# A two-layer AdaLN transformer on one core: the order of work in layer 1's feed-forward at its entry, pair change and end, and four operand rests on GpSimd

## What is computed

```python
h = _layernorm(x) * (1 + cb) + sb
g = (h @ gate_w.T) * gate_s          # 1408 hidden units
u = (h @ up_w.T) * up_s
x = x + gb * (((silu(g) * u) @ down_w.T) * down_s)
```

## Time and profile before

| | |
|---|---|
| median of three runs | 1994.6 us |
| the profiled execution | 1995.5 us, its span 1993.7 us |
| TensorE (PE) busy | 1905.1 us, 96% of the span |
| VectorE (DVE), ScalarE (ACT), GpSimd (POOL) busy | 58%, 35%, 39% |
| granted TensorE clock, mean | 0.986 of 2.4 GHz |

### The profile page before, as it was taken

One profiled execution on the slowest core, in us unless ns is written; L12 is line 12 of the kernel. 1 busy time (PEld: TensorE's weight loads), 2 busy tenths in 40 slices (PEclk: granted clock), 3 DMA queues, 4 the chain that ended last, 5 costly groups with the idle time before them and its releaser, 6 DMA issues. The chain is left out here.

```text
span 1993.7 us, 26372 instructions
## 1 busy us (share of the span) xinstructions
PE 1905.1 (96%) x9936; PEld 1367.3 (69%) x9936; DVE 1163.8 (58%) x1948; ACT 707.2 (35%) x1275; POOL 775.3 (39%) x730
## 2 busy tenths in 40 slices
PE   7999999999999999899999999998998878998998
PEld 5677555544555545788888888887886667776887
DVE  5466877666666733854434443445333767777776
ACT  4221355545555564521111111114221244343332
POOL 1122778788776589200000000002001556664662
PEclk9999999999999999999999999999999989999999
DMA  9852422322321203200001010002000011111211
GB/s 326 267 150 107 97 54 55 86 55 55 86 45 33 60 19 99 69 33 32 32 1 32 32 32 1 1 19 74 6 6 11 22 32 53 54 48 43 95 54 48
DMA packets 80783, 120.83 MB, mean 61 GB/s; under 512 B 7008, under 2 KB 38768, under 8 KB 80624
## 3 DMA queue, kind: packets, MB, share of 16 engines
q1 hardware_dynamic: 73200, 93.96, 16.5%
q0 software_dynamic: 7456, 25.18, 4.2%
HBM read 93.68 MB, written 25.44 MB: 60 GB/s over the span
## 5 line engine op out<-in xcount | busy, mean ns | idle before, releaser
L1795 DVE TENSOR_REDUCE part_max<-banks 128x1 f32<-128x512 f32 (+2 forms) x640 | 357.0, 614 | 149.3 <-PE banks L1767 91.0
L2320 ACT ACTIVATE probs<-banks 128x512 f32<-128x512 f32 (+3 forms) x640 | 311.0, 539 | 269.0 <-PE banks L2235 133.4
L1767 PE MATMUL banks<-kst,qst 96*128 96x512 f32 (+2 forms) x640 | 261.4, 417 | 12.1 <-DVE part_max L1795 9.7
L2231 PE MATMUL banks<-qst,kst 98*128 98x512 f32 (+2 forms) x640 | 251.4, 413 | 0.7 <-ACT probs L2320 0.6
L1429 POOL TENSOR_TENSOR w_lo<-early_weights,w_hi 128x512 fp32r<-128x512 f32 x4 | 5.1, 1302 | 544.1 <-ACT w_hi L1403 544.1
L763 DVE TENSOR_TENSOR tokens_b<-banks,tokens_b 128x512 f32<-128x512 f32 x64 | 44.3, 691 | 251.6 <-ACT tokens_b L678 251.6
L2181 POOL TENSOR_TENSOR early_weights<-probs 128x512 f32<-128x512 f32 (+2 forms) x152 | 160.6, 1089 | 56.4 <-ACT probs L2320 56.0
L2181 POOL TENSOR_TENSOR pairs_own<-probs 128x512 f32<-128x512 f32 (+2 forms) x152 | 157.3, 1068 | 63.4 <-ACT probs L2320 63.2
L678 ACT ACTIVATE tokens_b<-banks 128x512 f32<-128x512 f32 x64 | 38.2, 597 | 395.7 <-PE banks L229 395.7
L2231 PEld LDWEIGHTS banks<-qst,kst 98*128 98x128 f32 x640 | 123.6, 194 | 64.3 <-issue 49.0
L1767 PEld LDWEIGHTS banks<-kst,qst 96*128 96x128 f32 x640 | 123.5, 193 | 59.9 <-DVE part_max L1795 46.7
(11 more groups left out here) (251 smaller groups left out, 4211.9 us busy)
## 6 DMA issues: line engine op xcount, KB each, us to landing
tokens_a<-in_L_wmod SPq DMA_DIRECT2D x12, 1024.0 KB, 7.1
qst<-q_hi SPq DMA_DIRECT2D x32, 256.0 KB, 5.7
kst<-k_hi SPq DMA_DIRECT2D x32, 256.0 KB, 8.3
tokens_b<-in_down_wt SPq DMA_DIRECT2D x10, 512.0 KB, 3.7
q_hi<-qk_out_hi POOLq DMA_DIRECT2D x16, 256.0 KB, 3.4
q_lo<-qk_out_lo POOLq DMA_DIRECT2D x16, 256.0 KB, 3.4
k_hi<-qk_out_hi POOLq DMA_DIRECT2D x16, 256.0 KB, 4.1
k_lo<-qk_out_lo POOLq DMA_DIRECT2D x16, 256.0 KB, 4.3
```

The source lines that it names most:

```text
L1767: mm = nc.tensor.matmul(dst[:, 0:wide], qst[n % QS][0:BIASROW, h, P * t:P * t + P], kst[(NB * g + c) % KS][0:BIASROW, h, 0:wide], start=Tr ...
L1795: nc.vector.tensor_reduce(part_max[:, n % 2, ht, c:c + 1], max_bank(slot)[:, 0:wide], AX_X, ALU.max).then_inc(max_read, 1)
L2231: mm = nc.tensor.matmul(dst[:, c0:512], kst[ck % KS][0:BIASROW + 2, h, at:at + P], qst[n % QS][0:BIASROW + 2, h, c0:512], start=True, stop ...
L2320: nc.scalar.activation(probs[:, q % PS, h, c0:512], score_bank(sh)[:, c0:512], ACT.Exp, scale=SCALE).then_inc(exp_done, 1)
```

## The change

Entry: ScalarE makes both context hi's of a step of the loop before the square root of the previous block, not after it. VectorE multiplies both halves of `more_vector` before the statistics, not one before and one after z. TensorE turns blocks 0 and 1 as before, but block 2 in two halves behind g(0,0) and g(0,1), and block 3 in two halves behind g(0,5) and g(0,6) (before: block 2 ahead of g(0,0), block 3 behind g(0,3)). ScalarE makes unit 0's weight hi's ahead of rows(1), the snapshot of unit 0 ahead of operand 5, and VectorE makes rests 3, 2 and 4 of pair 0 earlier. Token sums 2 and 3 change places. The loads of unit 1's weights wait for six rests and the four token sums.

Segments: the lone unit is now the first of a pair (units 0; 1 and 2; ... 9 and 10). In the last unit its four down tiles are placed one, one and two.

Pair change: ScalarE's hi's for pair 1 are spread over the end of unit 10 and the start of unit 11. VectorE makes rests 0, 1 and 2 of pair 1 at three later places of unit 10, and GpSimd makes rests 3, 4, 5 and 6, between its weight rests for units 11 and 12, with a semaphore of their own.

```diff
-            def tensor(self, pe, b, first=0):
+            def tensor(self, pe, b, first=0, end=KT):
...
-            FIRST_ORDER = (0, 1, 6, 3, 4, 2, 5)
+            FIRST_ORDER = (0, 1, 6, 3, 2, 4, 5)
...
-                return SEGS * p + c // 2, c % 2
+                return (SEGS * p + 1 + (c - 1) // 2, (c - 1) % 2) if c else (SEGS * p, 0)
...
+                if u == UNITS - 1:
+                    return (tiles[:1], tiles[1:2], tiles[2:])
...
-                    sp.wait_ge(b_ready, 7)
+                    sp.wait_ge(b_ready, 6)
+                    sp.wait_ge(t_step, 4)
...
                             for i in range(3):
                                 Stage.weight_lo_gpsimd(pool, u + 1, i)
+                                if u == NCH - 1 and i:
+                                    Stage.operand_lo_gpsimd(pool, 1, i + 2)
+                                if u == NCH and i < 2:
+                                    Stage.operand_lo_gpsimd(pool, 1, i + 5)
...
+                def operand_lo_gpsimd(pool, p, j):
+                    pool.wait_ge(b_hi_s, op_at[p][j] + 1)
+                    nc.gpsimd.tensor_tensor(b_lo[:, j, :, :], operand(p, j), b_hi[:, j, :, :], ALU.subtract).then_inc(b_rest_g, 1)
...
-                        if u % NCH == 0:
+                        if u == NCH and j >= 3:
+                            pe.wait_ge(b_rest_g, j - 2)
+                        elif u % NCH == 0:
                             pe.wait_ge(b_ready, op_at[p][j] + 1)
...
                         for j in range(4):
                             gate_up(u, j)
-                        if u == 0:
-                            last_norm()
+                            if u == 0 and j < 2:
+                                turn(NB - 2, j)
...
                         gate_up(u, 5)
+                        if u == 0:
+                            turn(NB - 1, 0)
...
                         gate_up(u, 6)
+                        if u == 0:
+                            turn(NB - 1, 1)
...
                         add_trunk2(u)
-                        if u == NCH:
-                            for j in (5, 6):
-                                Stage.operand_lo_vector(dve, 1, j)
                         add_gate1_part(u)
-                        if u == NCH - 1:
-                            for j in range(4):
-                                Stage.operand_lo_vector(dve, 1, j)
...
                         add_up1(u)
+                        if u == NCH - 1:
+                            Stage.operand_lo_vector(dve, 1, 0)
                         for q, t in middle:
                             add_x(q, t)
                         if u == NCH - 1:
-                            Stage.operand_lo_vector(dve, 1, 4)
+                            Stage.operand_lo_vector(dve, 1, 1)
...
                         hidden_lo(u, 0)
+                        if u == NCH - 1:
+                            Stage.operand_lo_vector(dve, 1, 2)
...
-                    if b:
+                    if 0 < b < NB - 1:
                         norm.tensor(pe, b - 1)
...
                 for b in range(NB):
-                    if b:
-                        norm.std_scalar(act, b - 1)
                     if b + 1 < NB:
                         out_p.hi_scalar(act, 2 * b + 2)
                         out_p.hi_scalar(act, 2 * b + 3)
+                    if b:
+                        norm.std_scalar(act, b - 1)
...
                     if b == 2:
-                        rows_scalar(act, 1)
-                        ffn.operand_hi_scalar(act, 0, 6)
                         used(act)
                         for i in range(4):
                             ffn.weight_hi_scalar(act, 0, i)
-                        ffn.operand_hi_scalar(act, 0, 3)
-                        ffn.operand_hi_scalar(act, 0, 4)
+                        rows_scalar(act, 1)
+                        for j in (6, 3, 2, 4):
+                            ffn.operand_hi_scalar(act, 0, j)
...
                     if b + 1 < NB:
                         more_vector(dve, b + 1, 0)
+                        more_vector(dve, b + 1, 1)
+                    if b == NB - 1:
+                        ffn.operand_lo_vector(dve, 0, 3)
                     if b:
                         statistics(dve, b - 1)
-                    if b + 1 < NB:
-                        more_vector(dve, b + 1, 1)
+                    if b == NB - 1:
+                        ffn.operand_lo_vector(dve, 0, 2)
+                    if b:
+                        norm.z_vector(dve, b - 1)
                     out_p.add_vector(dve, 2 * b)
```

More of the change, by code:

```diff
@@ L174, in first_tensor @@
                             last.then_inc(self.turned, 1)
-            def tensor(self, pe, b, first=0):
+            def tensor(self, pe, b, first=0, end=KT):
                 pe.wait_ge(self.z_ready, TB * (b + 1))
-                for k in range(first, KT):
+                for k in range(first, end):
                     i = KT * b + k
@@ L860, in segment @@
                 p, c = divmod(u, NCH)
-                return SEGS * p + c // 2, c % 2
+                return (SEGS * p + 1 + (c - 1) // 2, (c - 1) % 2) if c else (SEGS * p, 0)
             def chunks_of(q):
                 s = q % SEGS
-                return range(2 * s, min(2 * s + 2, NCH))
+                return range(2 * s - 1, 2 * s + 1) if s else range(1)
             def last_unit(q):
@@ L1012, in source_ready @@
                 def source_ready(engine, p, j):
-                    step = {3: 1, 4: 2, 2: 3, 5: 4}.get(j)
+                    step = {3: 1, 2: 2, 4: 3, 5: 4}.get(j)
                     if step:
@@ L1062, in tensor @@
                     for u in range(UNITS):
-                        first, middle, last = place_of(down_tiles(u))
+                        first, middle, last = place_of(u)
                         for j in range(4):
                             gate_up(u, j)
-                        if u == 0:
-                            last_norm()
+                            if u == 0 and j < 2:
+                                turn(NB - 2, j)
                         for q, t in first:
@@ L1113, in scalar @@
                             silu(u - 1, 1)
-                        snapshot(u)
-                        if u:
+                            Stage.snapshot_scalar(act, u)
                             hidden_hi(u - 1, 1)
@@ L1268, in tensor @@
                         out_p.tensor(pe, 2 * b + part)
-                    if b:
+                    if 0 < b < NB - 1:
                         norm.tensor(pe, b - 1)
-                ffn.tensor(pe, lambda: norm.tensor(pe, NB - 1))
+                ffn.tensor(pe, lambda b, half: norm.tensor(pe, b, first=2 * half, end=2 * half + 2))
             def scalar(act):
@@ L1302, in statistics @@
                 norm.stats_vector(dve, b)
-                norm.z_vector(dve, b)
             def vector(dve):
```

39 lines of the change are left out of this document (21 added, 18 removed).

## The result

The changed kernel took 1998.28 us (median of 20 runs, 1993.80 to 2002.72), the kernel before 1994.82 us (20 runs, 1990.42 to 1999.59). The ratio is 1.0022 with a 95% interval of 1.0014 to 1.0029: 3.5 us slower by the medians and some 4.4 by the ratio, inside the 0.3% that was called "the same". The forecast was 2001.4 us, 6.8 us slower. The sign was right, the size was one and a half to two times too large.

The account below looks back on a forecast made before the run. TensorE alone bounds the steady feed-forward; elsewhere it waits, partly because VectorE and GpSimd take turns. +12.4 - 1.0 - 0.8 - 3.8 = +6.8 us on 1995.5 gives 2002.3, less 0.9 to the median: 2001.4 us, range 1989 to 2006.

Parts of the forecast that it names:

- late entry: Start of the kernel up to unit 3: turns and rests come later, +12.4 us in all (bounds +1, +15).
- pair change: Units 10 to 13: g(11,2) stalls 5.2 us for rest 2, 2.8 of clock, four small stalls 3.8; -0.8 us.
- the end: Last segment, now two units: more cover, one stall of 0.4 us, no clock loss; -3.8 us.
- units 3 to 9: Feed-forward units: one stall of about 1 us where two waits made 2.1 us; -1.0 us (bounds -2, +1).
- Square roots, turn(0): Entry, block 0: std(0) moves behind hi(5), so turn(0) starts at 1584.6, 3.6 us late.
- z(1): Entry, block 1: takes turns with GpSimd's weight rests, 5.4 us; turn(1) starts at 1609.25, 11.0 us later.
- Out(7) to turn(3): Entry, blocks 2 and 3: out(7) ends at 1626.6, z(2) at 1630.9, turn(3) at 1648.0, +11.4 us.
- rest 5's wait for a hi: Entry, VectorE: rest 5 waits for a hi behind rows(2) and the snapshot, so z(3) comes about 1643.8.
- Units 1 and 2: From turn(3) to unit 3: g(1,0) waits 3.05 us, g(3,0) comes 37.2 us after turn(3); +0.95 us.
- first rival: Pair change: rest 2 precedes GpSimd's rest 3, g(11,2) stalls 1.5 us, entry loses 10; 1993.2 us, chance 0.24.
- The second: Rival: no turns matter, z(1) under 2.5 us; entry +1.3, pair change -7.8; 1983.3 us, chance 0.12.
- The third: Rival at the pair change: GpSimd's four rests are the new bound, g(11,5) and g(11,6) wait; 2004 us, chance 0.08.

Follow-up runs that it names:

- Experiment 1: The changed kernel with ScalarE's square root std(b-1) between the two context hi's, not behind both: 1991.33 us, ratio 0.9986 to the kernel before.
- experiment 2: The changed kernel with unit 0's four weight hi's back behind rows(1) and operand hi 6, square roots still late: 2001.50 us, ratio 1.0036.
- Experiment 9: The changed kernel with ScalarE's wait for the scales moved from directly ahead of the first silu to ahead of unit 0's snapshot: 1996.57 us, ratio 1.0011.
- experiment 3: The changed kernel with the whole entry of before, new segments and new pair change kept: 1990.87 us, ratio 0.9976.
- experiment 5: The kernel of Experiment 1 with VectorE's rest 2 of pair 1 moved ahead of unit 10's first hidden product: 1991.39 us, ratio 0.9983.
- experiment 10: The kernel of Experiment 1 with ScalarE's wait for the scales moved ahead of unit 0's snapshot: 1990.33 us, ratio 0.9976.

## Why the prediction was right, and where it wasn't

The direction and the main mechanism were right: a late entry that the pair change and the end don't pay for. The time also had luck in it. The trace came out 3.7 us below the sum (3.1 against 6.8), and that is an entry 2.9 us and a pair change 2.0 us better than forecast, less 1.15 us for units 3 to 9, which the sum had wrong the other way. The table load, which stood in no term, hid part of the entry's error. Of the three classes "slower" had the best chance, 0.48, and "the same" came, at 0.38.

**Square roots, turn(0): right.** Forecast 1584.6, measured 1584.03 + 0.58; forecast wait 3.4 us, measured 3.46. Experiment 1 shows the cause.

**z(1): mechanism right, the price of a turn wrong.** The forecast was 5.4 us (four times 0.54 and three GpSimd instructions), measured 4.22, and turn(1) came at 1607.9, not 1609.25. I added whole lengths, where a turn costs 1.41 us and not 1.82: by these lengths the two overlap by some 0.4 us at each change-over. The rows for it were at hand: twelve bias adds beside z took 16.77 us, 1.40 each, with four z among them in 5.28, 1.32 each. Experiments 1 and 2 show that GpSimd's rests lengthened z(1): it takes 1.92 and 1.91 us where they aren't beside it, in 1 with ScalarE's hi(7) beside it.

The Trainium skill's rule (SBUF — State Buffer, "two separate sides") would have had z(1) at 1.92 us if the lock stayed with a queued run of VectorE's. The single tiles show a change of turn after each instruction. That the lock is held for a whole instruction, as the Trainium skill has it, agrees with them: each tile after the first ends 0.3 us behind the GpSimd instruction beside it.

**Out(7) to turn(3): the main error, 2.6 us too much with the above.** Out(7) ended at 1625.3 + 0.6, forecast 1626.6, after a wait of 2.52 us. The cause stands just beside the forecast one: rest(7) took its turns (3.41 us beside the token sums), but what TensorE waited for was the add behind it (L373). The 2.6 us can be followed through the traces:

- Rows(1) ended at 1612.1 + 0.6, 1.2 us ahead of forecast; that is the z(1) error carried on.
- From there to the end of z(2) it took 16.25 us, forecast 17.0: 0.75 less. I priced a token sum and a rest at 2.40 + 1.22 = 3.6 us, and two sums with rests beside them started 3.21 us apart (1614.70, 1617.91). Three such turns would explain 1.2 us, more than there is.
- From z(2) to z(3) it took 11.1 us, forecast 12.9: 1.8 less. The step that failed is rest 5's wait for a hi. VectorE worked with next to no gap from z(2) on, and rest 5 followed the statistics directly, as its row has no wait:

```profile
1634.81 1.22 DVE L1036 TENSOR_TENSOR w_b_lo<-w_t,w_b_hi 128x1024 fp32r<-128x1024 f32 x1
```

- Against these stood the table load, which was not in the sum at all: from z(3) to the end of turn(3) it took 5.3 us, forecast 4.2. Experiment 9 gives 1.35 us for the load.

**Units 1 and 2: right.** g(1,0) waited 2.88 us, forecast 3.05. The stretch grew by 0.6, forecast 0.95; in experiment 3 the segments alone make 1.3.

**Units 3 to 9: wrong.** I expected one wait of about 1 us for L1191 in place of two (2.1 us). There are two, 0.27 and 1.63 us, where before had 0.49 and 1.62. Shifting the segments moved the two meetings of down rests and token sum to other units and left them as long (3.92 and 3.91 us for two rests, at 1696.64 and 1728.88; 3.92 in the earlier trace rows). The step that failed is that one of the two would go; what the earlier trace rows says of a meeting was right.

**Pair change: the step was right, its gain 2.0 us larger than forecast.** g(11,2) waited for a rest of VectorE, and none of g(11,3) to g(11,6) for GpSimd, as forecast. The wait was 4.14 instead of 5.2, the clock 2.4 instead of 2.8, the four small ones 0.99, 0.48, 1.11 and 0.62, 3.2 instead of 3.8. Rest 2 was done 21.8 us after unit 10's start, not 22.9: probably turns that were priced whole once more (argued from the same rows; experiment 5 shows only that these instructions do take turns). One reading of the kernel before was off: ahead of the adds for which TensorE waited 5.83 us stood four rests, not five, and ahead of these VectorE had waited 3.99 us for ScalarE's hi's. My first rival had a wait of 1.5 us at g(11,2). Its 6.6 us don't follow from its own terms: 12.5 less 1.5 and 3.8 is 7.2. Experiment 5, which gets rest 2 in early by another way, says that little would have come of it: rest 2 done early pushes the hidden chain behind it.

**End: right.** -3.7 against -3.8, one gap, no loss of clock.

**Rivals.** The second, that no turns matter, had its own mark: z(1) under 2.5 us. It was 4.22. The third, GpSimd's rests as a new bound, did not come: no product of the changed kernel waits for them. Experiment 5 shows it appearing, 1.47 us at g(11,5). The first got the entry's size nearly (10, measured 9.4), but by luck: it has a z or rest(7) get its turn at once, and z(1) took its turns in the forecast's order while rest(7) took 3.41 us. The turns were cheaper, not sooner.

## What to carry to other kernels

A tiny instruction that others wait for (here a square root of 0.20 us) belongs at the place where its input is ready and not behind work that waits for a slower engine: its busy time says nothing of what it costs, and its place alone made TensorE wait 3.46 us at each of two blocks (experiment 2). When two engines take turns, price a turn by a row in which they did so over many instructions, not by adding two lengths. And a wait that is removed from one instruction on an engine with a full list is found again at the next one; sum over the whole stretch, from one product to a later one, before calling it a gain.

## What the runs showed of the hardware

- Even an instruction on 128x4 waits for the GpSimd instruction that is under way: VectorE's L147, 0.17 us elsewhere, took 1.95 us beside a token sum in experiment 10 and ended with it (1616.78 and 1616.75):

```profile
1614.83 1.95 DVE L147 TENSOR_SCALAR n_ve<-n_mv 128x4 f32<-128x4 f32 x1
...
1614.36 2.39 POOL L973 TENSOR_TENSOR w_t<-tokens_b,w_t 128x1024 f32<-128x1024 f32 x1
```

- An ACT_TABLE_LOAD can stand behind a wait of the activation that it serves. Then it isn't hidden, though ScalarE idles in front of it (5.64 us here). With two waits ahead of the activation it stood so (1640.79), with one it ran ahead of the wait (1635.35 in experiment 9); that this is the rule was not tested further.
- Waits of 4.1 us at g(11,2) stood in seven of the kernels. The next matmul ran at once at the lower clock in some (0.76 us long in the changed kernel), at full clock in others (0.47 in experiment 1, where matmuls of 0.63 us began only four matmuls later). From the wait of 1.63 us at g(6,3) to unit 14 all of them took 127.3 to 127.4 us nevertheless. What sets the clock's place was not tested.
